# A vision transformer's attention with the layer norm folded into the weights and a new order of its eight slots per pair

## The reference, cut to what matters

```
for i in range(4):
    y = layernorm(h, ln1_w[i], ln1_b[i])
    q, k, v = split(y @ qkv_w[i] + qkv_b[i])          # 8 heads of 16
    attn = softmax(q @ k.T * 16 ** -0.5)              # 197 x 197 per image and head
    h = h + ((attn @ v) @ proj_w[i] + proj_b[i])
    y = layernorm(h, ln2_w[i], ln2_b[i])
    h = h + (gelu(y @ fc1_w[i] + fc1_b[i]) @ fc2_w[i] + fc2_b[i])
```

## Time and profile before

| | |
|---|---|
| median of 3 runs | 5173.65 us (5172.24 to 5180.15) |
| profiled execution | 5158.09 us, its span 5156.3 us |
| busy: PE, DVE, ACT, POOL | 4016.1 (78%), 3192.7 (62%), 2017.0 (39%), 1581.0 us (31%) |
| mean granted TensorE clock | 0.875 |
| one layer (from the first `a_stats` row of layer 1 to that of layer 2) | 207.3 to 1124.5 us: 917.2 us, of which attention 737.2 |

### The profile page before, as it was taken

How to read it: one execution, slowest core, us unless ns; L and a number is a source line. 1 busy time by engine, 2 the same in 40 slices (tenths; PEclk the granted TensorE clock), 3 DMA queues, 4 the chain that set the end, 5 groups by cost and what they waited for, 6 DMA issues and landing times. The chain is left out here.

```text
span 5156.3 us, 96498 instructions
## 1 busy us (share of the span) xinstructions
PE 4016.1 (78%) x30842; PEld 3007.8 (58%) x30842; DVE 3192.7 (62%) x8237; ACT 2017.0 (39%) x3340; POOL 1581.0 (31%) x1608
## 2 busy tenths in 40 slices
PE   9588888757888875788887678888778878797784
PEld 9566666535666654566665456666553346565563
DVE  1367776556777755677774567676557758797411
ACT  0045454424455542355454335444433334332231
POOL 0011111331122133111112311111245546426586
PEclk9788888978888888788888868888899999899887
DMA  7444444014444400444440044444100002223243
...
DMA packets 455969, 341.19 MB, mean 66 GB/s; under 512 B 70659, under 2 KB 440171, under 8 KB 455595
## 3 DMA queue, kind: packets, MB, share of 16 engines
...
...
## 5 line engine op out<-in xcount | busy, mean ns | idle before, releaser
L528 DVE TENSOR_REDUCE a_neg_max<-a_S 99x4 f32<-99x788 f32 x1024 | 997.1, 974 | 548.6 <-PE a_S L300 544.5
L442 ACT ACTIVATE a_probs<-a_St 99x792 f32<-99x792 f32 (+1 forms) x1024 | 849.4, 830 | 620.9 <-PE a_St L315 619.6
L300 PE MATMUL a_S<-a_k_st,a_q_st 96*99 96x197 bf16 x4096 | 636.3, 286 | 485.8 <-DVE a_neg_max L528 265.3
L300 PEld LDWEIGHTS a_S<-a_k_st,a_q_st 96*99 96x99 bf16 x4096 | 457.1, 147 | 567.8 <-DVE a_neg_max L528 315.0
L315 PE MATMUL a_St<-a_q_st,a_k_st 99*99 99x198 bf16 (+1 forms) x4096 | 607.4, 277 | 43.0 <-ACT a_probs L442 41.5
L498 POOL TENSOR_TENSOR a_ve<-a_mv,eps 99x4 f32<-99x4 f32 x128 | 25.9, 202 | 2001.2 <-DVE a_mv L589 2001.2
L315 PEld LDWEIGHTS a_St<-a_q_st,a_k_st 99*99 99x99 bf16 (+1 forms) x4096 | 463.7, 143 | 185.9 <-issue 118.0
L330 PE MATMUL a_O<-a_probs,a_v_aug 99*32 99x198 f32 (+1 forms) x8192 | 521.6, 372 | 0.2
L448 ACT ACTIVATE a_o_sb<-a_O 128x396 f32<-128x396 f32 x256 | 128.3, 501 | 571.0 <-PE a_O L330 570.5
L330 PEld LDWEIGHTS a_O<-a_probs,a_v_aug 99*32 99x32 f32 (+1 forms) x8192 | 261.7, 118 | 110.3 <-issue 19.7
L506 POOL TENSOR_TENSOR a_parts<-a_res,a_parts 128x792 bf16<-128x792 f32 x128 | 216.2, 1689 | 355.4 <-ACT a_parts L487 355.4
...
## 6 DMA issues: line engine op xcount, KB each, us to landing
...
spill_q<-a_parts SPq DMA_DIRECT2D x384, 99.0 KB
spill_k<-a_parts SPq DMA_DIRECT2D x384, 99.0 KB
a_k_st<-spill_k SPq DMA_DIRECT2D x128, 297.0 KB, 4.2
a_q_st<-spill_q SPq DMA_DIRECT2D x128, 297.0 KB, 6.3
a_k_st<-spill_k SPq DMA_DIRECT2D x128, 198.0 KB, 4.7
a_q_st<-spill_q SPq DMA_DIRECT2D x128, 198.0 KB, 6.7
a_k_st<-spill_k SPq DMA_DIRECT2D x128, 99.0 KB, 5.0
```

The source lines that it names most:

```text
L300: mm = nc.tensor.matmul(S[0:TC, j // 2, j % 2 * TB:j % 2 * TB + NTOK], q_st[p][0:SPLIT, head, b * TB + c * TC:b * TB + (c + 1) * TC], k_st ...
L442: nc.scalar.activation(probs[0:keys, u % 4, :].rearrange("p (x t) -> p x t", x=2), St[0:keys, :, 0:2 * TB], ACT.Exp).then_inc(s["probs"], 1)
L528: nc.vector.tensor_reduce(out.rearrange("p (x y) -> p x y", x=2), S[0:TC, :, 0:2 * TB].rearrange("p x (y t) -> p x y t", y=2)[:, :, :, 0:N ...
```

## The change

The scale and the mean of the layer norm move into the weights: `load_layer` multiplies the rows of the q, k, v and first MLP weights by the norm's weight, subtracts from each column its mean (a product with a matrix of 1/128), and adds the norm's bias times the weights to the biases; the bias of v goes through the projection's weights into that bias. So `xn` becomes one product `h * rstd` without the mean (POOL in attention, DVE in the MLP), `yT` becomes a plain copy, and v is copied by ACT.

q and k come out of PE into one f32 buffer `q_k` (ACT, with their biases), and all four steps of the split, like the four of the maxima's, run on POOL; the maxima are split before they are transposed. One matmul then transposes the three parts, DVE copies them to `max_rows`, SP sends them on. POOL's program is no longer a loop.

Each step has eight slots; each has 4 matmuls of scores, 4 of turned scores and one or two other groups. The units of the scores are 5 to 7 of pair i+1 and 0 to 4 of pair i+2. The front is made earlier: `xn` and k of pair i+5, q and its parts of i+4, v of i+3, `bn_stats` of i+6. The projection is that of pair i-2. `yT`, `neg_max`, `max_rows` and `oT` have more than one buffer. On the other engines ten steps at the start (-6 to 3) and ten at the end (24 to 33) are written out, with twenty between in the loop.

Twelve columns of blanks are cut from the diff's left where there are that many, some waits of the first steps (`peeled`) are left out, and only the new side of the long rewritten parts is shown.

```diff
+    pe.wait_ge(s["w_scale"], 2)
+    nc.tensor.matmul(mean[:, 0:3 * D], g.all_mean[:], q_k_v, start=True, stop=True).then_inc(s["w_mean"], 1)
+    nc.tensor.matmul(mean[:, 512:512 + 2 * D], g.all_mean[:], w1, start=True, stop=True).then_inc(s["w_mean"], 1)
...
+    nc.vector.tensor_scalar(q_k_v, q_k_v, g.ln1_w, None, ALU.mult).then_inc(s["w_scale"], 1)
+    nc.vector.tensor_scalar(w1, w1, g.ln2_w, None, ALU.mult).then_inc(s["w_scale"], 1)
+    nc.vector.tensor_tensor(q_k_v, q_k_v, mean[:, 0:3 * D], ALU.subtract).then_inc(s["w_centre"], 1)
...
+    def body(i, p, even, live):
+        now, nxt, then, last = live(0), live(1), live(2), live(-1)
+        def slot(j):
+            if j < 3 and nxt:
+                scores(i + 1, p + 1, even, 5 + j)
+            if j >= 3 and then:
+                scores(i + 2, p + 2, even, j - 3)
+            if now:
+                scores_t(i, p, even, j)
+        slot(0)
+        if last:
+            pv(i - 1, p - 1, 1, 1)
+        slot(1)
+        if last:
+            oT_turn(i - 1, 0)
+        if live(-2):
+            wait(pe, s["oT"], 2 * (i - 1))
+            wait(pe, s["k_f"], upto(i + 5))
+            for t in range(4):
+                mm = nc.tensor.matmul(M0[0:TC, t * D:(t + 1) * D], oT[p % 2][:, t * TC:(t + 1) * TC], g.wp,
+                                      start=True, stop=True)
+            mm.then_inc(s["proj"], 1)
+        slot(2)
         if now:
+            pv(i, p, 0, 0)
+        if live(5):
+            wait(pe, s["xn"], i + 6)
+            wait(pe, s["max_copied"], i + 1)
+            for t in range(4):
+                mm = nc.tensor.transpose(M2[:, t * TC:(t + 1) * TC], xn[:, t, :], g.ident[0:TC, 0:TC])
             mm.then_inc(s["turned"], 1)
+        slot(3)
         if last:
             o_turn(i - 1, 1)
+        if live(4):
+            wait(pe, s["h_done"], i - 1)
+            nc.tensor.matmul(M0[:, 0:PW], g.wq, yT[p][:], start=True, stop=True).then_inc(s["q"], 1)
+        slot(4)
+        if nxt:
+            wait(pe, s["max_split"], 4 * (i + 2))
+            wait(pe, s["yT"], upto(i + 6))
+            nc.tensor.matmul(M2[0:96, 0:TC], max_parts[:].rearrange("p k n -> p (k n)"), ident[:],
+                             start=True, stop=True).then_inc(s["max_turned"], 1)
         if now:
+            pv(i, p, 0, 1)
+        slot(5)
         if last:
             oT_turn(i - 1, 1)
+        if live(3):
+            wait(pe, s["q_f"], upto(i + 5))
+            for t in range(4):
+                mm = nc.tensor.matmul(M0[0:TC, t * D:(t + 1) * D], yT[(p + 3) % 4][:, t * TC:(t + 1) * TC], g.wv,
                                       start=True, stop=True)
             mm.then_inc(s["v"], 1)
+        slot(6)
         if now:
             pv(i, p, 1, 0)
+        slot(7)
+        if now:
             o_turn(i, 0)
+        if live(5):
+            wait(pe, s["yT"], i + 6)
+            wait(pe, s["v_aug"], i + 4)
+            nc.tensor.matmul(M0[:, 0:PW], g.wk, yT[(p + 1) % 4][:], start=True, stop=True).then_inc(s["k"], 1)
...
+        if live(4):
+            wait(act, s["k"], i + 5)
+            wait(act, s["lo"], i + 4)
+            nc.scalar.activation(q_k[:, 1, :], M0[:, 0:PW], ACT.Identity, bias=g.bk).then_inc(s["k_f"], 1)
...
+        if live(5):
+            wait(act, s["turned"], i + 6)
+            wait(act, s["v"], i + 2)
+            nc.scalar.activation(yT[(p + 1) % 4][:], M2[:, 0:PW], ACT.Copy).then_inc(s["yT"], 1)
...
+            nc.scalar.activation(v_aug[(p + 3) % 4][:, :, :, 0:HD],
+                                 M0[0:TC, :].rearrange("p (t h e) -> p t h e", t=4, e=HD),
+                                 ACT.Copy).then_inc(s["v_aug"], 1)
...
+            wait(pool, s["rstd"], i + 6)
+            wait(pool, s["turned"], i + 5)
+            nc.gpsimd.tensor_tensor(xn[:], g.h[0:TC, bass.ds((i + 5) * 4, 4), :],
+                                    rstd[:].unsqueeze(2).to_broadcast([TC, 4, D]),
+                                    ALU.mult).then_inc(s["xn"], 1)
+        if live(1):
+            n, big = 4 * (i + 1), neg_max[(p + 1) % 2]
+            wait(pool, s["row_max"], 8 * (i + 2))
+            wait(pool, s["max_turned"], i + 1)
+            nc.gpsimd.tensor_copy(max_parts[:, 0, :], big[:]).then_inc(s["max_split"], 1)
+            wait(pool, s["max_split"], n + 1)
+            nc.gpsimd.tensor_tensor(max_res[:], big[:], max_parts[:, 0, :], ALU.subtract).then_inc(s["max_split"], 1)
+            wait(pool, s["max_split"], n + 2)
+            nc.gpsimd.tensor_copy(max_parts[:, 1, :], max_res[:]).then_inc(s["max_split"], 1)
+            wait(pool, s["max_split"], n + 3)
+            nc.gpsimd.tensor_tensor(max_parts[:, 2, :], max_res[:], max_parts[:, 1, :],
+                                    ALU.subtract).then_inc(s["max_split"], 1)
         if live(4):
+            wait(pool, s["k_f"], i + 5)
+            wait(pool, s["q_f"], i + 5)
+            wait(pool, s["part_wr"], 96 * (i + 4))
+            nc.gpsimd.tensor_copy(parts[:, 0, :, :], q_k[:]).then_inc(s["hi"], 1)
+            wait(pool, s["hi"], i + 5)
+            nc.gpsimd.tensor_tensor(q_k[:], q_k[:], parts[:, 0, :, :], ALU.subtract).then_inc(s["res"], 1)
+            wait(pool, s["res"], i + 5)
+            nc.gpsimd.tensor_copy(parts[:, 1, :, :], q_k[:]).then_inc(s["mid"], 1)
+            wait(pool, s["mid"], i + 5)
+            nc.gpsimd.tensor_tensor(parts[:, 2, :, :], q_k[:], parts[:, 1, :, :], ALU.subtract).then_inc(s["lo"], 1)
+    steps(body, looped=False)(pool)
...
+            wait(dve, max_rd[(p + 1) % 2], 48 * (even + (p + 1) // 2))
+            nc.vector.tensor_copy(max_rows[(p + 1) % 2][:], M2[0:96, 0:TC]).then_inc(s["max_copied"], 1)
...
-            nc.scalar.activation(yT[p][:], Y[p][:, 0:PW], ACT.Identity, bias=g.ln2_b,
-                                 scale=g.ln2_w).then_inc(s["m_yT"], 1)
+            nc.scalar.activation(yT[p][:], Y[p][:, 0:PW], ACT.Copy).then_inc(s["m_yT"], 1)
...
-            for t in range(4):
-                x = nc.vector.tensor_scalar(xn[p][:, t, :], g.h[0:TC, bass.ds((i + 2) * 4 + t, 1), :]
-                                            .rearrange("p o d -> p (o d)"), mv[p][:, t, 0:1],
-                                            rstd[p][:, t, :], ALU.subtract, ALU.mult)
-            x.then_inc(s["m_xn"], 1)
+            nc.vector.tensor_tensor(xn[p][:], g.h[0:TC, bass.ds((i + 2) * 4, 4), :],
+                                    rstd[p][:].to_broadcast([TC, 4, D]), ALU.mult).then_inc(s["m_xn"], 1)
```

More of the change, by code:

```diff
@@ L215, in attention_phase @@
     with ExitStack() as ctx:
-        s = Sems(nc, ctx, "stats aggr var_eps rstd xn turned yT q_k v hi res mid lo v_aug "
-                 "part_wr stack_rd max_rd scores row_max max_turned max_parts scores_t probs pv "
+        s = Sems(nc, ctx, "stats aggr var_eps rstd xn turned yT q k v q_f k_f hi res mid lo v_aug part_wr stack_rd0 stack_rd1 "
+                 "max_rd0 max_rd1 scores row_max max_split max_turned max_copied scores_t probs pv "
                  "o_copied o_turned recip o_norm oT_turned oT proj h_bias h_done ones")
@@ L355, in _, with peeled @@
-                pe.wait_ge(s["ones"], 8)
-                def body(i, p, live):
-                    now, nxt, then, front, last = live(0), live(1), live(2), live(3), live(-1)
-                    if now:
-                        scores_t(i, p, 0)
-                    if nxt:
-                        scores(i + 1, (p + 1) % 4, 4)
-                    if last:
-                        pv(i - 1, (p - 1) % 4, 1, 1)
-                    if front:
-                        wait(pe, s["xn"], i + 4)
-                        wait(pe, s["max_parts"], 4 * (i + 1))
+                def peeled(i, *waits):
+                    if isinstance(i, int):
+                        for name, value in waits:
+                            wait(pe, s[name], value)
@@ L407, in body @@
-                    if then:
-                        scores(i + 2, (p + 2) % 4, 0)
-                    if now:
-                        pv(i, p, 0, 1)
-                        scores_t(i, p, 5)
-                    if then:
-                        scores(i + 2, (p + 2) % 4, 1)
-                    if front:
-                        wait(pe, s["h_done"], i)
-                        nc.tensor.matmul(M1[:, 0:PW], g.wq, yT[:], start=True, stop=True).then_inc(s["q_k"], 1)
-                        wait(pe, s["oT"], 2 * i)
-                        nc.tensor.matmul(M2[:, 0:PW], g.wk, yT[:], start=True, stop=True).then_inc(s["q_k"], 1)
@@ L460, in body @@
                     if last:
                         o_copy(i - 1, 1)
[L462 to L466 removed]
                     if now:
[L468 removed]
                         exp(i, 2)
                     if last:
[L471 removed]
+                        oT_copy(i - 1, p - 1, 0)
@@ L483, in body @@
-                    if now:
-                        exp(i, 6)
-                    if front:
-                        wait(act, s["res"], 2 * (i + 4))
```

(14 more changed lines are left out.)

327 lines of the change are left out of this document (151 added, 176 removed).

## The result

| | before | after |
|---|---|---|
| median of 4 runs | 5172.94 us (5165.98 to 5180.15) | 4392.49 us (4384.37 to 4398.38) |
| ratio, 95% interval | | 0.849 (0.847 to 0.851) |
| profiled execution, span | 5158.09, 5156.3 us | 4389.62, 4387.8 us |
| mean granted clock | 0.875 | 0.923 |

The kernel is 15% faster. Forecast was 4490 us, with a range of 4400 to 4750: the side is right, the time lies 7.5 us under the range.

What follows compares the result with a forecast made beforehand. Attention was taken to be bound by order, a late DMA and the low clock. Four layers of (- 168 + 1 + 6 - 5.5) gave - 666 us from 5158, so 4492 us, with a range of 4400 to 4750.

Steps and rivals of the forecast that it cites:

- What bounds the kernel: Attention steps before the change: bound by queue order, a late DMA and the low clock these cause, not one engine's work.
- TensorE's work: PE's matmuls in a new attention step: 15.0 us summed, 15.25 with small gaps, claimed as the floor.
- four tight waits: Waits in a new attention step with at most 0.6 us spare; forecast step 16.0 us, 5% over the floor.
- P: Length of one full attention step, forecast at 16.0 us; 27 such steps in each of four layers.
- 2764 + 108P: Rule for the whole program's time in us from the length of a full attention step; forecast 4492.
- Rival 1: Maxima's small DMAs queue behind a stack's reads in SP's queue; steps 17.3 to 17.5 us, 4650 us; chance 0.14.
- Rival 2: Low clock stays in attention as waits add up in one place; steps 19.3 us, 4850 us; chance 0.07.
- Rivals 3 and 4: POOL's slow casts bind attention steps: 15.3 to 21.8 us, chance 0.12; or slower than before, from 22.2 us, chance 0.03.
- c: Unknown price of one POOL cast of 128 x 792 in attention, taken as 1.3 us.
- The ring: `q_f`, POOL's four operations, `k_f`, projection, through single buffer `q_k`; above a cast price of 1.7 us, steps are 11.8 + 2c.
- M0's three waits: Buffer serving proj, q, v, k in turn: k, v and proj each fit their waits by only 0.25 to 0.55 us.
- The rest of the sum: Per layer outside full steps: `load_layer` + 6 us, start no change within 4, end + 1, MLP - 5.5.

Runs made afterwards that it cites:

- The run with the old order: Changed kernel's folded norm, MLP norm and layer loading, but attention's order and engine splits as in the kernel before: 5191.2 us, 1.005 of before.
- the best version: Changed kernel with one DMA for the maxima, their copy ahead of the next unit's row maxima, and q's reads behind that DMA: 4272.2 us, 0.826 of before.
- ACT's queue: Changed kernel with the maxima's copy ahead and one DMA for them, that DMA issued by ACT instead of SP: 4289.8 us, 0.833 of before.
- the run with six DMAs: Changed kernel with three more DMAs of the maxima's rows into a spare tile, also waited for: 4647.5 us (one run).
- three casts: Changed kernel with POOL's two casts from `q_k` each done three times: 4609.7 us (one run).

## Why the prediction was right, and where it was wrong

- *What bounds the kernel* (order, a late stack, and the clock that they cost): right. The run with the old order shows that saved work alone gains nothing (1.005).
- *TensorE's work, "that is 15.0, with small gaps between kinds 15.25 us. No step can be shorter"*: wrong, and this is the step that failed. The floor is 14.02 us, shown by steps that repeat it to the hundredth and by the window in which PE is never idle. In the best version the start-to-start distances of the groups add up to it without a rest. The missing 1.23 us by terms: transposes of the result 0.88 against 1.2, those back 0.34 against 0.6, gaps none against 0.25, the maxima 0.14 against 0.25, scores and products with v together 9.18 against 9.3, the rest and the rounding to 15.0 0.17. The big ones are those that I sized by columns and then rounded up (the text finds 0.5 for a transpose of the result, the sum takes 0.6), and the gaps. A row of before would have had the first at 0.51 (476.74 to 477.25). A sum called a floor must be made of the smallest distances seen, and the margins put on top once.
- *16.0 us, "5% over the floor"*: 0.75 us were added for four tight waits. Measured were 0.64, and the only wait of PE in those steps is the maxima's DMA; it is gone in the best version. So P was 1.34 us too long (16.0 against 14.66), 1.23 of it by the floor and 0.11 by the waits. Times 108 that is 145 us; by the rule 2764 + 108P, P = 14.66 gives 4347, and 4389.6 was measured. The 42 us of difference are the routed part (20), longer steps in layers 2 to 4 (some 25: their exponentials take 6 to 11 us more than layer 1's), and small terms either way.
- *Rival 1, the maxima's DMAs are late* (0.14): the wait came true at a third of its price, but not by the queue, as ACT's queue shows. I had 1.8 us to land behind the issue, from no row of such a DMA; it was 3.3 (488.89 to 492.14), and 2.1 at the least (last of six, in the run with six DMAs). My reason against it, "the reads are through before the maxima's data would move", is wrong: the last read landed at 491.3, 2.4 us after the three had been issued (488.89).
- *Rival 2* (low clock): no; 1.00 in the steps. The run with six DMAs has it at 0.95 from 320 to 700 us, with PE idle for 37 of 380.
- *Rivals 3 and 4* (POOL): no; c = 0.84. The ring is real: it shows at three casts, c of about 2.5, where P = 11.8 + 2c says 16.8 and the steps are 16.4. POOL is busy for some 9.4 us a step, not 12.0. My estimate of about 1 us, worked out from the Trainium skill ("GPSIMD Engine Reference", "Engine selection": about line rate with one input), was nearer to 0.84 than the 1.3 that I took.
- *M0's three waits within 0.25 to 0.55 us*: none shows in after. *The rest of the sum* (load, start, end, MLP): each within 1 us in layer 1. ACT's work of a step, 10.4 in the text, is 10.6 by its own terms; nothing hangs on it.
- *The range*: I gave 0.02 to "something under the floor", as if the floor had been measured. It was the least supported number in the text.
